# Moving one block of second multilayer products and its output norm from the next-to-last stage into the last stage of a graph layer kernel

## The chip, the cores and the metric

One core of one Trainium2 chip runs the whole program. The metric is the time of the program on the device in microseconds. The kernel before takes 388.86 us (median of three runs, 388.27 to 390.04).

## The reference, cut to what matters

Thirty-two graphs of 256 tokens with 128 features pass through two layers. Each adds its input and normalises over the features:

```
L0: h      = bn2(conv17(relu(bn1(conv1(x)))));  x_conv = relu(h + x)
    A      = exp(-|s_n - s_m|^2), s = x @ w_se.T + b_se;  x_nmp = A @ relu(x @ w_msg.T + b_msg)
    r, z   = sigmoid(...), n = tanh(...)        # gates from x_conv, x_nmp and x
    x1     = layernorm(x + (1 - z) * n + z * x)
L1: hidden = relu(((1 + eps) * x1 + adj @ x1) @ W1 + b1)
    x2     = layernorm(x1 + hidden @ W2 + b2)
```

The kernel masks A with adj. Everything is float32. The products that need its precision split each operand into a high and a low part and take three matmuls in place of one.

## The kernel before, in words

The graphs are worked in 8 groups of 4 (GROUPS, GB). A group has 1024 columns (4 graphs by 256 tokens), in two halves h = 0 and 1 of 512 columns, which fill one PSUM bank each. The eight banks are `fb` (two, "front"), `bb` (three, "back") and `cb` (three, "conv").

The order on each engine is written out by hand: `run` (line 416) calls `prologue`, then `steady(s, u, front)` for s = 1 to 7, then `last`. Stage s works on three groups at once. For `gb = s - 1` it does the back part: gates, first norm, aggregation, both multilayer products, second norm, store. For `gm = s` it does the front part: convolution, distances and `nmp`. For `gf = s + 1` it prepares the streams of the convolution. The loop of stages 2 to 5 is a hardware loop. Stage 7 has `front=False`: there is no group 8 to prepare. `last` does the back part of group 7. It cuts that group into three items (LAST_ITEMS): the whole half 0, and the two quarters (256 columns) of half 1. That shortens the chain at the end.

The names that the change touches, with the lines of the profile:

- `mlp2(g, h)` on TensorE (L1424) is the second multilayer product: 4 blocks by 2 halves of the hidden units, 8 matmuls in the code for each half of the group, which the trace shows as 16 instructions of 128x128. It writes the bank "out" from the tile `hid`, which is part of the tensor `tail`.
- `nmp(g, h)` on TensorE (L1335, tiles front<-amat,msg) is the message product. It needs the masked matrix (`mask` on POOL, L542) and the tile `msg`. `nmp_high` on ACT (L619) and `nmp_low` on DVE (L821) split its result into nmph and nmpl.
- `gates(g, u, h, c)` on TensorE (L1222): six matmuls of r from x and nmp, three of hn, three more of r from the convolution, nine of z and six of n. The r products wait for `nmp_low` (NL_READY). The convolution part of r waits for both `xconv_low` on DVE (L967, XCL_READY), the low part of relu(x + conv). That follows `inf_add` (L962) and `xconv_high` on ACT (L694).
- `add_b2` on POOL (L536) writes xn + b2 into `ot`, which is the last part of `tail`. `out_stats` on DVE adds the bank "out" (L1025), takes the statistics (L991, two instructions of 256 columns) and the variance (L995). `rsqrt` on POOL (L524) and `out_shift` on DVE (L1039) follow, then `out_norm` on ACT (L703, one instruction for each of 4 blocks) and `store` on SP (L456).
- `aggregate` (L1335, tiles adjT,xn), `y_transpose` (L1386), `y_apply` (L1013), `h_high`, `h_low` (L619, L821) and `hidden` (ACT L710) are steps of the last group around the moved work.

Engines wait only on counting semaphores, and each executes its own queue in order. In stage 7, TensorE's queue ends with `mlp2(6, 0)`, `mlp2(6, 1)`, `nmp(7, 0)`, `nmp(7, 1)`. DVE's ends with

```
pair1_add(gm, 0); pair1_add(gm, 1); out_stats(gb, 0); xconv_low(gm, 0); out_stats(gb, 1)
nmp_low(gm, 0); inf_add(gm); nmp_low(gm, 1); xconv_low(gm, 1); out_shift(gb, 0); out_shift(gb, 1)
```

Of the kernel before, what the change touches and what calls it, by code (L numbers as in the profile page):

```python
# [11 lines left out]
EPS = 1e-5  # L12
# [83 lines left out]
def gnn_kernel(nc, t, out):  # L96
# [10 lines left out]
    with ctx:  # L107
# [70 lines left out]
        stats = sb("stats", [P, 2, PAIRS, BLK, 3])  # L178
        rstd = sb("rstd", [P, 2, PAIRS, BLK])
        shift = sb("shift", [P, PAIRS, BLK])  # L180
# [261 lines left out]
        def _(sp):  # L442
# [6 lines left out]
            def store(g, h, c=None):  # L449
# [6 lines left out]
                done(sp.dma_start(dst, ot[:, h, q, :].rearrange("p (b r) d -> p b (r d)", r=PAR)), STORED[h])  # L456
# [18 lines left out]
            def steady(s, u, front):  # L475
# [20 lines left out]
        def _(pool):  # L496
# [35 lines left out]
            def add_b2(g, h, c=None):  # L532
                q = slice(part_blocks(c).start, part_blocks(c).stop)
                wait(pool, XN_READY, g, item(h, c) + 1)
                wait(pool, STORED[h], g - 1, 16)
                done(pool.tensor_tensor(ot[:, h, q, :], xn[:, h, q, :],  # L536
# [44 lines left out]
            def steady(s, u, front):  # L581
# [15 lines left out]
                rsqrt(1, gb, 1)  # L597
# [3 lines left out]
            def last(g, u):  # L601
# [15 lines left out]
        def _(act):  # L617
# [82 lines left out]
            def out_norm(g, h, c=None):  # L700
                wait(act, SHIFT_READY, g, item(h, c) + 1)
                for q in part_blocks(c):
                    last = act.activation(ot[:, h, q, :], ot[:, h, q, :], ACT.Identity, bias=shift[:, h, q:q + 1],  # L703
                                          scale=rstd[:, 1, h, q:q + 1])
                done(last, OT_READY)
# [57 lines left out]
            def steady(s, u, front):  # L763
# [38 lines left out]
            def last(g, u):  # L802
# [16 lines left out]
        def _(dve):  # L819
# [167 lines left out]
            def norm_stats(k, g, h, c, src):  # L987

                q0, q1 = part_blocks(c).start, part_blocks(c).stop
                for q in range(q0, q1, 2):  # L990
                    last = dve.bn_stats(stats[:, k, h, q:q + 2, :].rearrange("p q s -> p (q s)"),  # L991
# [3 lines left out]
                done(dve.tensor_scalar(rstd[:, k, h, q0:q1], stats[:, k, h, q0:q1, 2], 1.0 / D, (4 * EPS, EPS)[k],  # L995
# [6 lines left out]
            def out_block(h):  # L1002
                return lambda a, b: ot[:, h, a:b, :].rearrange("p q d -> p (q d)")
# [5 lines left out]
            def y_apply(g, h, c=None):  # L1009
                src = y_block(h, c)  # L1010
                wait(dve, RSTD[0], g, item(h, c) + 1)
                for q in part_blocks(c):
                    last = dve.tensor_scalar(xn[:, h, q, :], src(q, q + 1), stats[:, 0, h, q, 1:2], rstd[:, 0, h, q:q + 1],  # L1013
# [7 lines left out]
            def out_stats(g, h, c=None):  # L1021
                wait(dve, W2_FULL, g, item(h, c) + 1)
                wait(dve, XNB_READY, g, item(h, c) + 1)
                row = ot[:, h, :, :].rearrange("p k d -> p (k d)")[:, part(c)]
                done(dve.tensor_tensor(row, bank("out", h, c), row, ALU.add), V_READY)  # L1025
                wait(dve, V_READY, g, item(h, c) + 1)
                norm_stats(1, g, h, c, out_block(h))

            def out_apply(g, h, c):
                wait(dve, RSTD[1], g, item(h, c) + 1)  # L1030
                for q in part_blocks(c):
                    last = dve.tensor_scalar(ot[:, h, q, :], ot[:, h, q, :], stats[:, 1, h, q, 1:2],
                                             rstd[:, 1, h, q:q + 1], ALU.subtract, ALU.mult)
                done(last, LAST_READY)

            def out_shift(g, h, c=None):
                q = slice(part_blocks(c).start, part_blocks(c).stop)
                wait(dve, RSTD[1], g, item(h, c) + 1)
                done(dve.scalar_tensor_tensor(shift[:, h, q], stats[:, 1, h, q, 1], -1.0, rstd[:, 1, h, q],  # L1039
# [96 lines left out]
            def steady(s, u, front):  # L1136
# [36 lines left out]
                out_stats(gb, 0)  # L1173
                xconv_low(gm, 0)
                if front:
                    half_stream(gf)
# [4 lines left out]
                out_stats(gb, 1)  # L1181
                nmp_low(gm, 0)
                inf_add(gm)
                if front:
                    stream_low(gf, 2)
                nmp_low(gm, 1)
                xconv_low(gm, 1)
                out_shift(gb, 0)
                out_shift(gb, 1)

            def last(g, u):
# [12 lines left out]
                for h, c in LAST_ITEMS:  # L1204
                    h_low(g, h, c)
# [11 lines left out]
        def _(pe):  # L1217
# [128 lines left out]
            def gates(g, u, h, c=None):  # L1346
# [14 lines left out]
                if i == 0:  # L1361
                    wait(pe, V_READY, g - 1, 2)
# [39 lines left out]
            def mlp1(g, h, c=None):  # L1402
                i = item(h, c)
                for f in range(2):
# [135 lines left out]
```

How the kernel before makes its waits and increments, by code:

```python
        def wait(eng, name, g, j):  # L321
            s, per, first, missing = count[name]
            v = (g - first) * per + j - missing
            if not (isinstance(v, int) and v <= 0):
                eng.wait_ge(s, v)
# [131 lines left out]
            def prologue():  # L458
                sp.dma_start(first_w[:, :], t["first"]).then_inc(first_loaded, 16)
                sp.dma_start(xv[0][:, cols(0)], x_v[0, :, cols(0)]).then_inc(x_pair0_loaded, 16)
                done(sp.dma_start(xv[0][:, cols(1)], x_v[0, :, cols(1)]), X_LOADED)
                sp.dma_start(c2raw[:, 0:5, :], t["conv2"][:, 0:5, :]).then_inc(conv2_loaded, 16)
                sp.dma_start(c2raw[:, 5:9, :], t["conv2"][:, 5:9, :]).then_inc(conv2_loaded, 16)
                sp.dma_start(later_w[:, :], t["later"]).then_inc(later_loaded, 16)
                sp.wait_ge(conv2_loaded, 64)
                wait(sp, X_LOADED, 0, 16)
                load_x(1, 1)
                load_adj(0, 0)
                sp.dma_start(graw, t["gates"]).then_inc(gates_loaded, 16)
                wait(sp, A_READY, 0, 1)
                wait(sp, CONV_FULL[MINUS1], 0, 1)
                sp.wait_ge(w_low, w_count(MINUS1))
                load_adj(1, 1)
# [78 lines left out]
            def prologue():  # L552
# [7 lines left out]
                pool.memset(full(facthl[:, :, :, :]), 0.0).then_inc(factors_set, 1)  # L560
                pool.memset(fact[:, :, :, :], 1.0).then_inc(factors_set, 1)
                pool.wait_ge(exponent_set, 1)
                pool.wait_ge(bn_var_ready, 1)
```

## Time and profile before

| what | value |
|---|---|
| median of three runs | 388.86 us |
| the profiled execution's own time | 390.09 us |
| span of the profiled execution, first to last instruction | 388.3 us |
| TensorE (PE) busy | 363.9 us, 94% of the span |
| VectorE (DVE) busy | 327.9 us, 84% |
| ScalarE (ACT) busy | 231.5 us, 60% |
| GpSimd (POOL) busy | 223.3 us, 58% |
| mean granted TensorE clock | 0.986 of full speed |

The span leaves out 1.8 us of the execution's own time, before the first and behind the last instruction. The busy times overlap. Stage 7 ends and `last` begins at about 355 us of the span.

### The profile page before, as it was taken

The page shows a single profiled execution, that of the slowest core. Times are in us where ns is not written, and L with a number is a line of the kernel's source. Part 1 is how long each engine was busy: PE and PEld are TensorE (multiplying, and loading weights), DVE is VectorE, ACT ScalarE, POOL GpSimd, SP SyncE. Part 2 cuts the span into 40 slices and gives each one's busy share as a digit, 9 for nine tenths or more (in the row PEclk, how much of TensorE's full clock was granted, in tenths as well). Part 3 has the DMA queues.
Part 4 walks back from the last instruction along what each step waited for, and adds up shares of the span by engine and source line. Part 5 has one row for each costly group of instructions (what it writes and reads, how often), then busy time and mean ns, then how long its engine had stood idle before and what let it go on. Part 6 is the DMA issues. An engine that isn't in the chain of part 4 may idle for free.

```text
span 388.3 us, 6417 instructions
## 1 busy us (share of the span) xinstructions
PE 363.9 (94%) x2150; PEld 314.4 (81%) x2150; DVE 327.9 (84%) x669; ACT 231.5 (60%) x435; POOL 223.3 (58%) x195
## 2 busy tenths in 40 slices
PE   4969998899999999999999999999999999999974
PEld 1747866798888998989888898989888898988953
DVE  3999999999699986999689986999789986977564
ACT  4455345563866566673775667674676558472773
POOL 3346173698428763597437863597537863395342
PEclk9998998999999999999999999999999999999998
DMA  6500003130110210120100300130101201000011
GB/s 231 223 0 3 0 0 114 51 111 1 56 54 18 93 43 13 56 108 0 54 23 31 108 27 27 54 108 0 57 5 50 110 2 54 3 0 2 0 56 54
DMA packets 7991, 19.39 MB, mean 50 GB/s; under 512 B 672, under 2 KB 5024, under 8 KB 6944
## 3 DMA queue, kind: packets, MB, share of 16 engines
q1 hardware_dynamic: 7536, 18.50, 13.6%
q10 hardware_dynamic: 432, 0.59, 0.4%
q8 instruction: 13, 0.21, 0.2%
q14 instruction: 10, 0.08, 0.1%
HBM read 14.90 MB, written 4.19 MB: 49 GB/s over the span
## 4 chain that ended last, share of the span: by engine, by line
PE 60%; DVE 30%; issue 5%; DMA 2%; ACT 1%; POOL 1%; SPq 0%; DVEq 0%; ACTq 0%
PE back L1222 25%; PE conv L1222 17%; PE back L1335 6%; PE back L1424 3%; DVE stats L991 3%; DVE stl L821 3%; DVE tail L1025 2%; PE front L1307 2%; DMA tail<-in_conv_dram 2%; DVE nmpl L821 2%; DVE adjT L1087 2%; DVE wl L1044 2%; PE back L1386 2%; DVE sv L842 1%; PE front L1327 1%
## 5 line engine op out<-in xcount | busy, mean ns | idle before, releaser
L1222 PE MATMUL conv<-sth,wh 128*128 128x256 f32 x217 | 65.4, 301 | 2.0 <-DVE stl L821 1.9
L1222 PE MATMUL conv<-stl,wh 128*128 128x256 f32 x217 | 61.8, 285 | 0.0
L1222 PE MATMUL conv<-sth,wl 128*128 128x256 f32 x217 | 61.7, 284 | 0.0
L524 POOL TENSOR_TENSOR rstd<-rstd,minus_half 128x4 f32<-128x4 f32 (+1 forms) x34 | 38.7, 1138 | 34.0 <-DVE rstd L995 33.4
L542 POOL TENSOR_TENSOR amat<-amat,adjT 128x512 f32<-128x512 f32 x32 | 50.4, 1604 | 4.6 <-ACT amat L663 4.6
L529 POOL TENSOR_TENSOR xw<-xw,xv 128x512 f32<-128x512 f32 (+1 forms) x17 | 21.4, 1256 | 50.0 <-ACT xw L687 50.0
L1222 PEld LDWEIGHTS conv<-sth,wh 128*128 128x128 f32 x217 | 40.9, 189 | 4.7 <-DVE stl L821 1.8
L1222 PEld LDWEIGHTS conv<-stl,wh 128*128 128x128 f32 x217 | 41.0, 189 | 0.1
L1222 PEld LDWEIGHTS conv<-sth,wl 128*128 128x128 f32 x217 | 40.8, 188 | 0.0
L619 ACT ACTIVATE sth<-sv 128x272 fp32r<-128x272 f32 (+1 forms) x33 | 17.3, 523 | 33.6 <-DVE sv L842 21.5
L536 POOL TENSOR_TENSOR tail<-xn,later_w 128x512 f32<-128x512 f32 (+1 forms) x17 | 30.8, 1815 | 4.3 <-DMA out_dram<-tail 2.6
L550 POOL TENSOR_TENSOR adjT<-adjT,diag 128x256 f32<-128x256 f32 x32 | 28.4, 917 | 8.0 <-DVE diag L1133 8.0
L703 ACT ACTIVATE tail<-tail,shift,rstd 128x128 f32<-128x128 f32 x62 | 24.8, 481 | 12.7 <-DVE shift L1039 12.7
L510 POOL TENSOR_TENSOR sv<-vv 128x272 f32<-128x272 f32 x8 | 9.1, 1143 | 35.1 <-DVE vv L869 35.1
L1335 PE MATMUL front<-amat,msg 128*128 128x256 f32 x128 | 29.1, 379 | 0.0
L1335 PE MATMUL back<-adjT,xn 128*128 128x256 f32 x120 | 28.2, 387 | 0.8 <-DVE xn L1013 0.8
L1424 PEld LDWEIGHTS back<-later_w,tail 128*128 128x128 f32 x240 | 28.0, 192 | 0.6
L1424 PE MATMUL back<-later_w,tail 128*128 128x128 f32 x240 | 28.1, 275 | 0.0
L1335 PEld LDWEIGHTS front<-amat,msg 128*128 128x128 f32 x128 | 23.8, 190 | 2.9
L1335 PEld LDWEIGHTS back<-adjT,xn 128*128 128x128 f32 x120 | 22.0, 190 | 5.1 <-DVE xn L1013 1.5
L710 ACT ACTIVATE tail<-back,first_w 128x512 f32<-128x512 f32 (+1 forms) x30 | 20.5, 682 | 9.2 <-PE back L1222 8.9
L957 DVE TENSOR_TENSOR usum<-usum,pm 128x512 f32<-128x512 f32 x16 | 25.4, 1624 | 0.0
(225 smaller groups left out, 1028.1 us busy)
## 6 DMA issues: line engine op xcount, KB each, us to landing
adjT<-in_adj_dram SPq DMA_DIRECT2D x8, 1024.0 KB, 4.8
out_dram<-tail SPq DMA_DIRECT2D x15, 256.0 KB, 2.2
xv<-in_x_dram SPq DMA_DIRECT2D x7, 512.0 KB, 3.3
gbuf<-in_gates_dram SPq DMA_DIRECT2D x1, 576.0 KB, 6.5
tail<-in_conv_dram ACTq DMA_DIRECT2D x2, 256.0 KB, 3.7
xv<-in_x_dram SPq DMA_DIRECT2D x2, 256.0 KB, 5.0
later_w<-in_later_dram SPq DMA_DIRECT2D x1, 452.0 KB, 7.2
tail<-in_conv_dram SPq DMA_DIRECT2D x1, 320.0 KB, 5.3
```

Of the source, the lines that this page charges most:

```text
L524: done(pool.tensor_tensor(rstd[:, k, h, q], rstd[:, k, h, q], minus_half[:, q], ALU.pow), RSTD[k])
L529: done(pool.tensor_tensor(xw[:, h, part(c)], xw[:, h, part(c)], xv[u][:, part_cols(h, c)], ALU.mult), XWX_READY)
L536: done(pool.tensor_tensor(ot[:, h, q, :], xn[:, h, q, :], b2bc.unsqueeze(1).to_broadcast([P, len(part_blocks(c)), D]), ALU.add), XNB_READY)
L542: done(pool.tensor_tensor(amat[:, b, :, :], amat[:, b, :, :], adjT[u][:, b, :, :], ALU.mult), A_READY)
L550: done(pool.tensor_tensor(dg, dg, diag[:, :].unsqueeze(1).to_broadcast([P, PAR, P]), ALU.add), ADJE_READY)
L703: last = act.activation(ot[:, h, q, :], ot[:, h, q, :], ACT.Identity, bias=shift[:, h, q:q + 1], scale=rstd[:, 1, h, q:q + 1])
L710: done(act.activation(hid[:, h, f, part(c)], bank("hid", h, c, f), ACT.Relu, bias=vec[:, B1 + f:B1 + f + 1]), HID_READY)
L821: done(dve.tensor_tensor(dst, src, full(hi), ALU.subtract), name)
L957: done(dve.tensor_tensor(a, a, p1, ALU.add), PRE_READY)
L1222: ins = pe.matmul(bank, a, b, start=first and k == 0, stop=last and k == len(todo) - 1)
L1335: ins = pe.matmul(tile[:, k * N:(k + 1) * N], lhs(b, rm), rhs(b, rm), start=rm == 0, stop=rm == PAR - 1)
L1424: ins = pe.matmul(bank("out", h, c)[:, k * P:(k + 1) * P], hid[:, h, f, q * P:(q + 1) * P], w2[:, f, :], start=f == 0, stop=f == 1)
```

## The change

Half 1 of group 6 gives up its place in stage 7 for all that follows its hidden layer. Its second product (`mlp2`) is issued in `last`, behind the gates of group 7 and one transpose, and goes to the bank `cb[0]`. The final add, the statistics, the square root, the norm and the store of that half move into `last` as well. In stage 7 the two `xconv` splits and `inf_add` of group 7 come ahead of the add of half 0, and ahead of the `nmp` splits.

So that the output tile of half 1 stays with group 6 until it is stored, the two quarters of half 1 of group 7 get their output in the tile `msg`, which is free once `nmp(7)` is done, and a third row in `stats`, `rstd` and `shift`. These three tiles grow by 96, 32 and 16 bytes in each partition.

The diff, cut to its core:

```diff
-        stats = sb("stats", [P, 2, PAIRS, BLK, 3])          # rstd, shift likewise
+        stats = sb("stats", [P, 2, PAIRS + 1, BLK, 3])
+        def place(h, c):
+            return PAIRS if h == 1 and halved(c) else h
+        def held_back(g, h):
+            return isinstance(g, int) and g == GROUPS - 2 and h == 1
+        def out_tile(h, c):
+            return msg[:, :, :, :].rearrange("p r b d -> p (r b) d")[:, 0:BLK, :] if place(h, c) == PAIRS else ot[:, h, :, :]
 # SP
                 store(gb, 0)
-                store(gb, 1)
+                if front:
+                    store(gb, 1)
             def last(g, u):
+                store(g - 1, 1)
                 for h, c in LAST_ITEMS:
 # POOL
             def add_b2(g, h, c=None):
-                wait(pool, STORED[h], g - 1, 16)
+                if place(h, c) == h:
+                    wait(pool, STORED[h], g - 1, 16)
+                else:
+                    wait(pool, NMP_FULL, g, 2)
-                rsqrt(1, gb, 1)                             # steady
+                if front:
+                    rsqrt(1, gb, 1)
                     add_b2(g, h, c)                         # last
+                rsqrt(1, g - 1, 1)
 # ACT, steady
-                nmp_high(gm, 0)
                 if front:
+                    nmp_high(gm, 0)
                     stream_high(gf, 2)
-                nmp_high(gm, 1)
-                xconv_high(gm, 1)
+                    nmp_high(gm, 1)
+                    xconv_high(gm, 1)
+                else:
+                    xconv_high(gm, 1)
+                    nmp_high(gm, 0)
+                    nmp_high(gm, 1)
 # ACT, last
                 out_norm(g - 1, 0)
-                h_high(g, 0, WHOLE)
-                out_norm(g - 1, 1)
-                h_high(g, 1, 0)
-                h_high(g, 1, 1)
+                for h, c in LAST_ITEMS:
+                    h_high(g, h, c)
                 for h, c in LAST_ITEMS:
                     hidden(g, h, c)
+                out_norm(g - 1, 1)
 # DVE, steady, front=False
+                    inf_add(gm)
+                    xconv_low(gm, 0)
+                    xconv_low(gm, 1)
+                    out_stats(gb, 0)
+                    nmp_low(gm, 0)
+                    nmp_low(gm, 1)
+                    out_shift(gb, 0)
 # DVE, last
-                for h, c in LAST_ITEMS:
-                    h_low(g, h, c)
+                h_low(g, 0, WHOLE)
+                out_sum(g - 1, 1)
+                h_low(g, 1, 0)
+                h_low(g, 1, 1)
+                out_norm_stats(g - 1, 1)
+                out_shift(g - 1, 1)
 # PE
                 if i == 0:                                  # gates, before hn
-                    wait(pe, V_READY, g - 1, 2)
+                    wait(pe, V_READY, g - 1, 2 if c is None else 1)
+                    if c == WHOLE and f == 1:               # mlp1, before the second half of item 0
+                        wait(pe, V_READY, g - 1, 2)
                 wait(pe, HID_READY, g, 2 * i + 2)           # mlp2
+                if held:
+                    wait(pe, TZ_READY, g + 1, 3)
+                tile = cb[0] if held else bank("out", h, c)
                 mlp2(gb, 0)                                 # steady
-                mlp2(gb, 1)
+                if front:
+                    mlp2(gb, 1)
                 gates(g, u, 1, 1)                           # last
                 y_transpose(g, 1, 0)
+                mlp2(g - 1, 1)
                 aggregate(g, u, 0, WHOLE, (0,))
```

`out_sum` is the add of `out_stats`, and `out_norm_stats` the rest of it.

## Rows read from the trace of the kernel before

**Rows 1.** The page's first part: busy time of each engine.
```profile
PE 363.9 (94%) x2150; PEld 314.4 (81%) x2150; DVE 327.9 (84%) x669; ACT 231.5 (60%) x435; POOL 223.3 (58%) x195
```
**Rows 2.** The chain that ended last, 318 to 389 us: start, us, what.
```profile
348.17 3.57 PE back L1424 x32
```
**Rows 3.** Timeline of TensorE, 348 to 358 us: start, us, engine, line, operation.
```profile
348.01 3.73 PE L1424 MATMUL back<-later_w,tail 128*128 128x128 f32 x32
...
351.58 3.62 PE L1335 MATMUL front<-amat,msg 128*128 128x256 f32 x16
...
354.98 0.47 PE L1222 MATMUL back<-xh,wh 128*128 128x512 f32 x1
...
356.91 0.39 PE L1222 MATMUL back<-xh,wl 128*128 128x512 f32 x1
...
357.67 0.50 PE L1222 MATMUL back<-xch,wh 128*128 128x512 f32 x1 [0.37 <-DVE xcl L967]
```
**Rows 4.** Timeline of all engines, 368 to 372 us.
```profile
368.44 0.47 ACT L683 ACTIVATE gbuf<-conv,gbias 128x256 f32<-128x256 f32 x1 [0.58 <-PE conv L1222]
...
368.96 0.38 PE L1386 MATMUL conv<-ident_w,gbuf 128*128 128x128 f32 x2
...
369.50 1.36 DVE L1013 TENSOR_SCALAR xn<-back,stats,rstd 128x128 f32<-128x128 f32 x4
...
370.96 1.10 PE L1335 MATMUL front<-adjT,xn 128*128 128x256 f32 x4 [1.62 <-issue]
```
**Rows 5.** Timeline of DVE, 344 to 358 us.
```profile
350.00 0.69 DVE L1025 TENSOR_TENSOR tail<-back,tail 128x512 f32<-128x512 f32 x1 [2.76 <-PE back L1424]
...
351.60 0.69 DVE L967 SCALAR_TENSOR_TENSOR xcl<-usum,xch 128x512 fp32r<-128x512 f32 x1
...
354.14 0.69 DVE L821 TENSOR_TENSOR nmpl<-front,nmph 128x512 fp32r<-128x512 f32 x1 [0.26 <-ACT nmph L619]
...
356.48 1.14 DVE L967 SCALAR_TENSOR_TENSOR xcl<-usum,xch 128x512 fp32r<-128x512 f32 x1
```
**Rows 6.** Timeline of ACT, 348 to 354 us.
```profile
348.80 0.62 ACT L694 ACTIVATE xch<-usum 128x512 fp32r<-128x512 f32 x1
353.51 0.60 ACT L619 ACTIVATE nmph<-front 128x512 fp32r<-128x512 f32 x1 [4.09 <-PE front L1335]
```
**Rows 7.** Timeline of POOL, 341 to 358 us.
```profile
341.14 2.60 POOL L536 TENSOR_TENSOR tail<-xn,later_w 128x512 f32<-128x512 f32 x1 [0.24 <-DVE xn L1013]
343.70 5.93 POOL L542 TENSOR_TENSOR amat<-amat,adjT 128x512 f32<-128x512 f32 x4
351.77 1.39 POOL L524 TENSOR_TENSOR rstd<-rstd,minus_half 128x4 f32<-128x4 f32 x1 [2.14 <-DVE rstd L995]
...
354.94 3.27 POOL L550 TENSOR_TENSOR adjT<-adjT,diag 128x256 f32<-128x256 f32 x4
```
**Rows 8.** Timeline of all engines, 374 to 385 us.
```profile
374.09 1.27 POOL L536 TENSOR_TENSOR tail<-xn,later_w 128x512 f32<-128x512 f32 x1 [0.36 <-DMA out_dram<-tail]
...
376.33 0.42 DVE L821 TENSOR_TENSOR nmpl<-back,nmph 128x256 fp32r<-128x256 f32 x1 [0.29 <-ACT nmph L619]
...
376.41 0.39 PE L1222 MATMUL conv<-nmph,w1h 128*128 128x512 f32 x1
...
380.14 0.69 DVE L1025 TENSOR_TENSOR tail<-front,tail 128x512 f32<-128x512 f32 x1 [3.39 <-PE front L1424]
...
380.88 0.47 ACT L710 ACTIVATE tail<-back,first_w 128x256 f32<-128x256 f32 x1
...
383.17 2.41 ACT L703 ACTIVATE tail<-tail,shift,rstd 128x128 f32<-128x128 f32 x6 [1.82 <-DVE shift L1039]
```
**Rows 9.** The page's DMA issues: KB each, us from issue to landing.
```profile
out_dram<-tail SPq DMA_DIRECT2D x15, 256.0 KB, 2.2
```
**Rows 10.** The page's groups, weight loads: count | busy us, mean ns | idle before.
```profile
L1222 PEld LDWEIGHTS conv<-sth,wh 128*128 128x128 f32 x217 | 40.9, 189 | 4.7 <-DVE stl L821 1.8
...
L1424 PEld LDWEIGHTS back<-later_w,tail 128*128 128x128 f32 x240 | 28.0, 192 | 0.6
```

More of the change, by code:

```diff
@@ L701, in out_norm @@
                 wait(act, SHIFT_READY, g, item(h, c) + 1)
+                o, v = out_tile(h, c), place(h, c)
                 for q in part_blocks(c):
-                    last = act.activation(ot[:, h, q, :], ot[:, h, q, :], ACT.Identity, bias=shift[:, h, q:q + 1],
-                                          scale=rstd[:, 1, h, q:q + 1])
+                    last = act.activation(o[:, q, :], o[:, q, :], ACT.Identity, bias=shift[:, v, q:q + 1],
+                                          scale=rstd[:, 1, v, q:q + 1])
                 done(last, OT_READY)
@@ L989, in norm_stats @@
                 q0, q1 = part_blocks(c).start, part_blocks(c).stop
+                v = place(h, c)
                 for q in range(q0, q1, 2):
-                    last = dve.bn_stats(stats[:, k, h, q:q + 2, :].rearrange("p q s -> p (q s)"),
+                    last = dve.bn_stats(stats[:, k, v, q:q + 2, :].rearrange("p q s -> p (q s)"),
                                         src(q, q + 2).rearrange("p (q d) -> p d q", q=2))
@@ L1019, in h_low, with out_sum, out_norm_stats, out_stats @@
                 low(hl[:, h, part(c)], bank("agg", h, c), hh[:, h, part(c)], HL_READY)
-            def out_stats(g, h, c=None):
+            def out_sum(g, h, c=None):
                 wait(dve, W2_FULL, g, item(h, c) + 1)
                 wait(dve, XNB_READY, g, item(h, c) + 1)
-                row = ot[:, h, :, :].rearrange("p k d -> p (k d)")[:, part(c)]
-                done(dve.tensor_tensor(row, bank("out", h, c), row, ALU.add), V_READY)
+                row = out_tile(h, c).rearrange("p k d -> p (k d)")[:, part(c)]
+                src = cb[0][:, :] if held_back(g, h) else bank("out", h, c)
+                done(dve.tensor_tensor(row, src, row, ALU.add), V_READY)
+            def out_norm_stats(g, h, c=None):
                 wait(dve, V_READY, g, item(h, c) + 1)
-                norm_stats(1, g, h, c, out_block(h))
+                norm_stats(1, g, h, c, out_block(h, c))
+            def out_stats(g, h, c=None):
+                out_sum(g, h, c)
+                out_norm_stats(g, h, c)
             def out_apply(g, h, c):
                 wait(dve, RSTD[1], g, item(h, c) + 1)
+                o, v = out_tile(h, c), place(h, c)
                 for q in part_blocks(c):
-                    last = dve.tensor_scalar(ot[:, h, q, :], ot[:, h, q, :], stats[:, 1, h, q, 1:2],
-                                             rstd[:, 1, h, q:q + 1], ALU.subtract, ALU.mult)
+                    last = dve.tensor_scalar(o[:, q, :], o[:, q, :], stats[:, 1, v, q, 1:2], rstd[:, 1, v, q:q + 1],
+                                             ALU.subtract, ALU.mult)
                 done(last, LAST_READY)
@@ L1037, in out_shift @@
                 q = slice(part_blocks(c).start, part_blocks(c).stop)
+                v = place(h, c)
                 wait(dve, RSTD[1], g, item(h, c) + 1)
-                done(dve.scalar_tensor_tensor(shift[:, h, q], stats[:, 1, h, q, 1], -1.0, rstd[:, 1, h, q],
+                done(dve.scalar_tensor_tensor(shift[:, v, q], stats[:, 1, v, q, 1], -1.0, rstd[:, 1, v, q],
                                               ALU.mult, ALU.mult), SHIFT_READY)
@@ L1180, in steady @@
                     stream_low(gf, 1)
[L1181 to L1184, printed above, removed]
+                    out_stats(gb, 1)
+                    nmp_low(gm, 0)
+                    inf_add(gm)
                     stream_low(gf, 2)
[L1186 to L1189, printed above, removed]
+                    nmp_low(gm, 1)
+                    xconv_low(gm, 1)
+                    out_shift(gb, 0)
+                    out_shift(gb, 1)
+                else:
+                    inf_add(gm)
+                    xconv_low(gm, 0)
+                    xconv_low(gm, 1)
+                    out_stats(gb, 0)
+                    nmp_low(gm, 0)
+                    nmp_low(gm, 1)
+                    out_shift(gb, 0)
             def last(g, u):
@@ L1418, in mlp2 @@
                 i = item(h, c)
+                held = held_back(g, h)
                 wait(pe, HID_READY, g, 2 * i + 2)
[L1420 removed]
+                if held:
+                    wait(pe, TZ_READY, g + 1, 3)
+                elif c is not None:
                     wait(pe, (XN_READY, HL_READY, HID_READY)[i], g, (3, 3, 1)[i])
+                tile = cb[0] if held else bank("out", h, c)
                 for k, q in enumerate(part_blocks(c)):
                     for f in range(2):
[L1424 removed]
+                        ins = pe.matmul(tile[:, k * P:(k + 1) * P], hid[:, h, f, q * P:(q + 1) * P],
                                         w2[:, f, :], start=f == 0,
```

25 lines of the change are left out of this document (11 added, 14 removed).

## The prediction

> **What bounds the kernel now.** I began with the busy times [rows 1]: TensorE has 94% of the span, so work off its queue pays only where it has no hole to go into. The chain of waits came next [rows 2]. It holds the 32 instructions of the two second products of group 6, in front of the message product and the gates of group 7. Later it passes through all engines, to the last norms on ACT. The timelines of the two seams follow. TensorE at the start of the last group [rows 3]: it runs without a hole to 356.91, then stands for DVE's xcl. TensorE behind the last gates [rows 4]: two transposes at 368.96, then 1.62 us of nothing, until DVE has made xn (369.50 + 1.36 = 370.86). So there are 1.8 us of work ahead of the seam that needs no place there, and a hole of nearly that length 20 us later. The other engines' timelines [rows 5 to 7] say whether they can follow.
>
> **Part 1: the second product leaves stage 7.** The 32 instructions start at 348.01 and the message product at 351.58 [rows 3]: 3.57 / 32 = 0.112 us each. Sixteen go: 1.79 us. Is the message product free to start 1.79 us earlier, at 349.79? Its first half needs two masks and its second all four. POOL's four masks end at 343.70 + 5.93 = 349.63 [rows 7]. Yes. It takes 354.98 - 351.58 = 3.40 us [rows 3], so TensorE reaches the gates at 353.19.
>
> The gates' first products need the low part of the first message half. ACT makes the high part from 353.51 now [rows 6], so from 351.72, and ends it at 352.32. What is ahead of nmp_low on DVE is new: ACT's two xch (348.80 and 349.3, 0.62 each) let xcl start at about 349.45, and two xcl of 0.69 end at 350.74. Then out_stats, the add with its statistics and variance, holds DVE for 1.6 us (350.00 to 351.60), to 352.3 [rows 5]. nmp_low then ends at about 352.40 + 0.69 = 353.09, 0.1 us before TensorE asks. That is thin: 0 to 0.3 us could be lost here. Term: -1.79.
>
> **Part 2: the stall goes.** The gates' matmuls start (356.91 - 354.98) / 8 = 0.24 us apart, so the convolution part would start at 357.15. It starts at 357.67, and that first matmul after the pause takes 0.50 and not 0.39 [rows 3]: 0.52 + 0.11 = 0.63 us. With inf_add and both xcl ahead of out_stats, xcl is ready at 350.74, and TensorE comes to it at 353.19 + 9 x 0.24 = 355.35. The wait is over 4.6 us early, so the whole 0.63 goes. Next late would be the first message half, counted in part 1. The wait ahead of hn falls from two adds to one; that one ends at 351.4. Term: -0.63. Bounds: -0.63, or 0 if nmp_low takes the place of xcl.
>
> The second xcl takes 1.14 us and the first 0.69, of the same shape; during the second, POOL adds the diagonals (354.94 to 358.21) [rows 5, 7]. In the new order both xcl come before that work, but the first (349.45) meets the end of the last mask (349.63). At most 0.2 us is added to DVE's queue, and nmp_low slips by up to 0.1 us behind TensorE. The Trainium skill (SBUF — State Buffer, Who interferes with whom) says that a DVE instruction with two SBUF inputs contends with a GpSimd instruction that reads SBUF, and that whoever is first holds the pair for the whole instruction. By that rule the first xcl starts at 349.63; the trace agrees in the 1.14 against 0.69. The moved add reads PSUM and the statistics have one input, so by the same rule they don't slow POOL.
>
> **Part 3: the product in its new place.** It stands behind the two transposes and waits for tz of the last item, which ACT ends at 368.44 + 0.47 = 368.91, before the transposes start [rows 4]. So the wait is met. Nothing else is behind it but the aggregation, which waits for 370.86 anyway. In the times of before, the product starts at about 369.18, and 16 x 0.112 = 1.79 us later TensorE is free: 370.97, against 370.96 at which the aggregation starts now. Term: 0. Bounds: -0.1 (the aggregation's first matmul comes without a pause, as the 0.11 of part 2) to +0.3 (the slot is 1.62 and its edges are not sharp). If the cover were gone altogether it would be +1.79.
>
> **Part 4: the norm of the held half** (in times of before; the whole block shifts alike). DVE: the 0.69 us add goes between the low splits of items 0 and 1. At the worst it pushes the last split from 376.33 + 0.42 = 376.75 to 377.4, while TensorE has the second half of mlp1 of item 0 in front of it, from 376.41 for three matmuls of 0.24 [rows 8]. That second half waits for the add too, which stands behind one split of 0.69 [rows 5] and ends near 375.8. So mlp1 of item 1 may come 0.1 late, where TensorE still has slack: 0. Statistics and variance follow in some 0.9 us (1.6 less the add), to 377.7 or at worst 378.3; DVE stands until 380.14 [rows 8]. POOL: the add of item 0 ends at 374.09 + 1.27 = 375.36. The two quarter adds behind it no longer wait for the store and take as much together, to 376.6, or to 378.0 at the 2.60 of rows 7. The square root (1.39 [rows 7]) of the variance at 377.7 ends at 379.1 (at worst 379.7), the shift 0.2 later: before 380.14. ACT: the norm (4 x 0.40, from 2.41 / 6) goes behind the last hidden (380.88 + 0.47 = 381.35) and ends at 382.95. The chain asks for ACT at 383.17 [rows 8]: 0.2 us are spare. Term: 0; bounds 0 to +1.6 (ACT's four on the path). The norm's old place, among the high splits of group 7, is counted at nothing as well: TensorE waits for xn there.
>
> SP: the store of the held half goes ahead of the last three, issued at 383.0. SP's next issue is due when the norm of item 0 ends, at 383.17 + 4 x 0.40 = 384.8. The first lands 2.2 us later [rows 9], at 385.2, as the data of the next store begin. Term: 0; bounds 0 to +0.3. POOL's new wait, for the message product, is met: that ends before the gates start.
>
> **The sum.** -1.79 - 0.63 + 0 + 0 = -2.42 us. The profiled execution took 390.09, with a span of 388.3: it would be 387.7 and 385.9. That execution is 1.23 above the median of the three runs; on the median, 388.86 - 2.42 = 386.4. I say 386.5, for the 0.1 us that part 1 may lose. What a measurement can tell here is 0.5%, 1.94 us: the forecast is -0.62%, not far beyond it.
>
> **Rivals.**
> 1. *DVE becomes the bound at the seam.* nmp_low is behind two xcl and a whole out_stats now. If xcl take 1.14 each, and one waits for the mask, DVE is 1.1 later, nmp_low ends at 354.1, and TensorE stands 0.9 us (and 0.1 for the restart): 388.86 - 2.42 + 1.0 = 387.4. For it: only 0.1 us of slack. Against it: no POOL work besides the last 0.2 us of the mask.
> 2. *The tail takes it back.* The norm of the held half ends on the path: ACT's four instructions stand before the last norms. With all 1.6 us: 388.0. For it: 0.2 us of slack, and a wait of DVE on POOL ahead of the add of item 0. Against it: every step above fits with POOL at double time.
> 3. *The hole isn't a hole.* The product delays the aggregation in full: 388.86 - 0.63 = 388.2. Or the message product can't start earlier (masks): 388.2 as well. Against: 368.91, 370.86 and 349.63.
> 4. *Slower: the grown tiles.* xn and tail start 144 bytes later in each partition, in every stage, not only in the last. TensorE loads weights from tail in 240 instructions of 192 ns [rows 10]. If each took 10% more and it came through to the end, 240 x 0.019 = 4.6 us: 388.86 - 2.42 + 4.6 = 391.0. It decides from 2.42 / 240 = 10 ns on. Against: loads from another tensor take 189 ns, 3 ns less, so the place in memory shows little so far; but no row has the same tensor at two places.
>
> **Chances.** Forecast (-2.0 to -2.7): 0.68. Rival 1: 0.12 at full price. Rival 2: 0.10. Rival 3: 0.06. Rival 4: 0.04. The range 386.0 to 387.9 holds the forecast's, rival 1 and half of rival 2. Faster by over 0.5%: 0.72 (the forecast and a light form of rivals 1 and 2). Within 0.5%: 0.24. Slower: 0.04.
>
> **What would show it.** The message product follows 16 instructions of L1424 and starts near 349.8. No DVE xcl wait stands in front of TensorE at the gates, which start near 353.2, and their convolution part near 355.4. The other 16 of L1424 stand at about 366.8 with the aggregation right behind (about 368.6). The four L703 of the held half end before the shift of item 0, and the span is 385.9. I am wrong if nmpl releases TensorE at the gates by more than 0.3 us, if the aggregation comes over 0.3 us behind xn, or if ACT's first L703 of item 0 is started by ACT itself and not by DVE's shift. Gaps in stages 1 to 6 would mean rival 4.

## The result, and the profile after

The changed kernel takes 386.50 us (median of 6 runs, 386.14 to 386.63) against 389.07 us for the kernel before, run beside it (6 runs). The ratio is 0.993, with a 95% interval of 0.9918 to 0.9942: faster by 0.7%. The prediction was 386.5 us. The profiled execution took 386.43 us, with a span of 384.5 us. One run of all those reported here, one of e7 below, was in a slower state of the chip (408.35 us, granted clock 0.847) and is left out of its median.

The lines have moved: L1222, L1335, L1386, L1424 of before are L1266, L1379, L1430, L1474 now, and DVE's L967 and L1025 are L990 and L1050. The busy times hardly differ from [rows 1], since no work was removed:

```profile
PE 363.2 (94%) x2150; PEld 315.1 (82%) x2150; DVE 326.4 (85%) x669; ACT 232.1 (60%) x435; POOL 222.5 (58%) x195
```

The chain of waits has 16 instructions of L1474 ahead of the message product where [rows 2] has 32. The 21 matmuls of the gates behind it (r, hn and z of item 0) are one piece of TensorE: before, the chain left TensorE there for ACT's nmph and DVE's nmpl and xcl.

```profile
346.82 1.78 PE back L1474 x16
348.60 3.46 PE front L1379 x16
352.06 4.90 PE back L1266 x21
```

**The first seam**, which is where stage 7 hands over to the last group. The timeline of TensorE, to be read against [rows 3]. To compare two traces I take times from the start of the masks of group 7 on POOL, the last thing ahead of the change. It is 343.70 before [rows 7] and 342.35 here.

```profile
346.66 1.95 PE L1474 MATMUL back<-later_w,tail 128*128 128x128 f32 x16
348.44 3.62 PE L1379 MATMUL front<-amat,msg 128*128 128x256 f32 x16
351.83 0.47 PE L1266 MATMUL back<-xh,wh 128*128 128x512 f32 x1
...
354.01 0.39 PE L1266 MATMUL back<-xch,wh 128*128 128x512 f32 x1
```

| step of TensorE, from the masks' start | before | after | difference |
|---|---|---|---|
| message product starts | 7.88 | 6.09 | -1.79 |
| gates start | 11.28 | 9.48 | -1.80 |
| convolution part of r starts | 13.97 | 11.66 | -2.31 |
| first aggregation starts | 27.26 | 24.86 | -2.40 |
| end of the span | 44.57 | 42.17 | -2.40 |

There is no idle time in brackets at 354.01, and that matmul takes 0.39 and not 0.50. The timeline of DVE there, against [rows 5]:

```profile
345.99 0.48 DVE L985 SCALAR_TENSOR_TENSOR usum<-conv,sc,usum 128x256 f32<-128x256 f32 x1
348.10 1.33 DVE L990 SCALAR_TENSOR_TENSOR xcl<-usum,xch 128x512 fp32r<-128x512 f32 x2 [1.62 <-ACT xch L713]
349.35 0.68 DVE L1050 TENSOR_TENSOR tail<-back,tail 128x512 f32<-128x512 f32 x1
...
351.00 0.69 DVE L844 TENSOR_TENSOR nmpl<-front,nmph 128x512 fp32r<-128x512 f32 x1
```

Both xcl are done at 349.43, 4.6 us before TensorE wants them. nmpl ends at 351.69, and TensorE starts the gates at 351.83, 0.14 us later. That is not time to spare, as e5 shows below: in that run TensorE stands idle for nmpl, and it starts as far behind its end. nmpl itself starts 0.03 us behind the end of ACT's nmph (350.97), as in all traces but that of e5. POOL and ACT beside them, against [rows 6, 7]:

```profile
342.35 5.93 POOL L559 TENSOR_TENSOR amat<-amat,adjT 128x512 f32<-128x512 f32 x4
...
352.10 2.84 POOL L567 TENSOR_TENSOR adjT<-adjT,diag 128x256 f32<-128x256 f32 x4
```

```profile
350.37 0.60 ACT L638 ACTIVATE nmph<-front 128x512 fp32r<-128x512 f32 x1 [1.78 <-PE front L1379]
```

**The second seam**, behind the last gates. The timeline of all engines at the hole of [rows 4]. The product fills it. xn is ready at 367.10 (365.74 + 1.36), and the aggregation starts at 367.21, 0.11 us behind it. Before it was 0.10 us.

```profile
365.20 0.38 PE L1430 MATMUL conv<-ident_w,gbuf 128*128 128x128 f32 x2
...
365.42 1.95 PE L1474 MATMUL conv<-later_w,tail 128*128 128x128 f32 x16
...
365.74 1.36 DVE L1037 TENSOR_SCALAR xn<-back,stats,rstd 128x128 f32<-128x128 f32 x4
...
367.21 1.10 PE L1379 MATMUL front<-adjT,xn 128*128 128x256 f32 x4
```

**The tail**, the norms and stores at the end. The timeline of all engines, against [rows 8].

```profile
371.25 0.68 DVE L1050 TENSOR_TENSOR tail<-conv,tail 128x512 f32<-128x512 f32 x1
...
371.50 1.44 POOL L553 TENSOR_TENSOR msg<-xn,later_w 128x256 f32<-128x256 f32 x2
...
372.57 0.42 DVE L844 TENSOR_TENSOR nmpl<-back,nmph 128x256 fp32r<-128x256 f32 x1 [0.31 <-ACT nmph L638]
...
373.96 1.02 POOL L538 TENSOR_TENSOR rstd<-rstd,minus_half 128x4 f32<-128x4 f32 x1 [1.02 <-DVE rstd L1019]
375.01 0.16 DVE L1072 SCALAR_TENSOR_TENSOR shift<-stats,rstd 128x4 f32<-128x4 f32 x1 [1.13 <-POOL rstd L538]
...
377.47 1.64 ACT L723 ACTIVATE tail<-tail,shift,rstd 128x128 f32<-128x128 f32 x4
...
379.39 1.65 ACT L723 ACTIVATE tail<-tail,shift,rstd 128x128 f32<-128x128 f32 x4 [0.29 <-DVE shift L1072]
...
381.83 0.85 SPq L467 DMA_DIRECT2D out_dram<-msg  x2
```

The held half's add (371.25) doesn't move the last low split: it starts 372.57 - 342.35 = 30.22 behind the masks and 376.33 - 343.70 = 32.63 before, 2.41 earlier like all the rest. DVE waits 1.13 us for POOL's root and has the shift at 375.17, 1.2 us before the add of item 0 (376.38). ACT ends the held norm and still waits 0.29 us for DVE's shift of item 0. From start to start there is more: ACT's norms of one row follow each other 0.38 us apart, so item 0 could start at 377.47 + 1.54 = 379.01, and starts at 379.39. That is 0.38 to 0.39 us to spare.

**What is not of the change.** The two profiled spans (388.27 and 384.52) differ by 3.75 us, 2.40 of them behind the masks' start. The other 1.35 are there from the start-up on. The first stores of the two, in SP's timeline, are 1.31 apart, before first:

```profile
98.37 1.93 SPq L456 DMA_DIRECT2D out_dram<-tail  x2
```

```profile
97.06 1.93 SPq L467 DMA_DIRECT2D out_dram<-tail  x2
```

From there to the masks both take 245.3 us. The experiments, whose code is the same up to stage 7 (e3 and all kernels with the change have the three tiles grown), show this start-up anywhere in between, and beyond. The granted clock is not what moves it: its mean is 0.998 in e10, whose masks start 1.06 us later than those of this profile with 0.989. What moves it stays open. From 340 to 381 us the granted clock is 1.00 in all thirteen traces.

### The profile page after: what moved, and what is told of

Read it like the earlier page. It is cut to its first block, busy times and chain, and to the rows that moved or that the text cites. A ratio compares the mean times of both kernels' runs of the same rounds, so it can differ in the third digit from the quotient of the medians.

```text
span 384.5 us, 6418 instructions
## 1 busy us (share of the span) xinstructions
PE 363.2 (94%) x2150; PEld 315.1 (82%) x2150; DVE 326.4 (85%) x669; ACT 232.1 (60%) x435; POOL 222.5 (58%) x195
## 4 chain that ended last, share of the span: by engine, by line
PE 61%; DVE 30%; issue 5%; DMA 1%; ACT 1%; POOL 1%; SPq 0%; DVEq 0%; ACTq 0%
PE back L1266 26%; PE conv L1266 17%; PE back L1379 6%; DVE stats L1015 3%; PE back L1474 3%; DVE stl L844 3%; DVE tail L1050 2%; PE front L1351 2%; DVE wl L1077 2%; DVE adjT L1120 2%; PE back L1430 2%; DVE sv L865 1%; DVE nmpl L844 1%; DMA tail<-in_conv_dram 1%; PE front L1371 1%
## 5 line engine op out<-in xcount | busy, mean ns | idle before, releaser
L1266 PE MATMUL conv<-sth,wh 128*128 128x256 f32 x217 | 65.4, 301 | 1.9 <-DVE stl L844 1.8
L1266 PE MATMUL conv<-stl,wh 128*128 128x256 f32 x217 | 61.8, 285 | 0.0
L1266 PE MATMUL conv<-sth,wl 128*128 128x256 f32 x217 | 61.7, 284 | 0.0
L1266 PEld LDWEIGHTS conv<-sth,wh 128*128 128x128 f32 x217 | 40.9, 189 | 4.6 <-DVE stl L844 1.7
L1266 PEld LDWEIGHTS conv<-stl,wh 128*128 128x128 f32 x217 | 41.1, 189 | 0.1
L1266 PEld LDWEIGHTS conv<-sth,wl 128*128 128x128 f32 x217 | 40.8, 188 | 0.0
L553 POOL TENSOR_TENSOR tail<-xn,later_w 128x512 f32<-128x512 f32 x15 | 29.4, 1959 | 2.0 <-DVE xn L1037 1.7
L1379 PE MATMUL front<-amat,msg 128*128 128x256 f32 x128 | 29.1, 379 | 0.0
L1379 PE MATMUL back<-adjT,xn 128*128 128x256 f32 x120 | 28.2, 387 | 0.8 <-DVE xn L1037 0.8
L1474 PEld LDWEIGHTS back<-later_w,tail 128*128 128x128 f32 x224 | 26.2, 192 | 0.6
L1474 PE MATMUL back<-later_w,tail 128*128 128x128 f32 x224 | 26.3, 275 | 0.0
L1379 PEld LDWEIGHTS front<-amat,msg 128*128 128x128 f32 x128 | 23.8, 190 | 2.9
L1379 PEld LDWEIGHTS back<-adjT,xn 128*128 128x128 f32 x120 | 22.0, 190 | 5.1 <-DVE xn L1037 1.5
```

Of the source, the lines that this page charges most:

```text
L553: done(pool.tensor_tensor(out_tile(h, c)[:, q, :], xn[:, h, q, :], b2bc.unsqueeze(1).to_broadcast([P, len(part_blocks(c)), D]), ALU.add), ...
L1266: ins = pe.matmul(bank, a, b, start=first and k == 0, stop=last and k == len(todo) - 1)
L1379: ins = pe.matmul(tile[:, k * N:(k + 1) * N], lhs(b, rm), rhs(b, rm), start=rm == 0, stop=rm == PAR - 1)
L1474: ins = pe.matmul(tile[:, k * P:(k + 1) * P], hid[:, h, f, q * P:(q + 1) * P], w2[:, f, :], start=f == 0, stop=f == 1)
```

## The experiments

The measure is the distance from the start of the masks of group 7 to the end of the span, in one profiled execution each; the median of the timed runs stands beside it. "The kernel after" in the diffs is the changed kernel.

| kernel | masks start | first aggregation, from the masks | end, from the masks | median us (runs) |
|---|---|---|---|---|
| before | 343.70 | 27.26 | 44.57 | 389.07 (6) |
| after | 342.35 | 24.86 | 42.17 | 386.50 (6) |
| e1, reorder only | 343.60 | 26.65 | 43.95 | 388.61 (12) |
| e2, product only | 343.06 | 25.47 | 42.76 | 387.27 (6) |
| e3, grown tiles | 342.88 | 27.27 | 44.56 | 389.13 (12) |
| e4, product twice | 342.98 | 26.64 | 43.70 | 388.52 (12) |
| e5, DVE later | 342.65 | 25.97 | 43.27 | 387.62 (4) |
| e6, norm earlier | 342.92 | 24.85 | 42.16 | 386.76 (4) |
| e7, norm twice | 344.15 | 24.86 | 43.31 | 387.97 (7) |
| e8, last quarters on DVE | 343.19 | 24.81 | 41.89 | 386.62 (6) |
| e9, a quarter of the product | 343.90 | 24.83 | 42.14 | 387.16 (4) |
| e10, the changed kernel again | 343.41 | 24.84 | 42.14 | 386.30 (5) |
| e11, e8 again | 342.72 | 24.84 | 41.91 | 386.13 (5) |

The kernel before ran beside them all, with medians of 389.01 to 389.11. Two traces of one kernel agree in the distance within 0.03 us (after and e10, e8 and e11). The masks' start varies by 1.8 us, and medians of one kernel differ by 0.2 us (after and e10) and 0.5 us (e8 and e11), so the distance decides where a few tenths matter.

**e1: the order of stage 7 alone.**

```diff
 # the kernel before, ACT and DVE in stage 7 (front=False)
+                    xconv_high(gm, 1); nmp_high(gm, 0); nmp_high(gm, 1)
+                    inf_add(gm); xconv_low(gm, 0); xconv_low(gm, 1)
+                    out_stats(gb, 0); out_stats(gb, 1); nmp_low(gm, 0); nmp_low(gm, 1)
```

> The kernel before, with only the order of ACT and DVE in stage 7 changed: inf_add and both xconv splits first, both out_stats next, the nmp splits last. The second product of half 1 stays in stage 7. Distance from the start of the masks of group 7 on POOL to the end of the span (44.6 us before, 42.15 after the change). My theory: the wait of TensorE for xcl goes and nothing else, so 0.63 us less, 43.95, with no pause ahead of the gates' convolution part; in the time, 0.6 us less, too small for a verdict. Rival (the nmp splits behind the out_stats become the wait): the gates start late by 0.5 us or more and the distance stays at 44.6.

Measured: 43.95, 0.62 us less than before; the time's ratio is 0.9988 (0.9978 to 0.9998). DVE's timeline shows both xcl ahead of the two adds. The second term of the sum stands alone, at its size.

```profile
349.36 1.32 DVE L971 SCALAR_TENSOR_TENSOR xcl<-usum,xch 128x512 fp32r<-128x512 f32 x2 [1.63 <-ACT xch L694]
350.60 0.68 DVE L1029 TENSOR_TENSOR tail<-back,tail 128x512 f32<-128x512 f32 x1
```

**e2: the product alone.**

```diff
 # the kernel after, ACT and DVE in stage 7
-                    xconv_high(gm, 1); nmp_high(gm, 0); nmp_high(gm, 1)
+                    nmp_high(gm, 0); nmp_high(gm, 1); xconv_high(gm, 1)
-                    inf_add; xconv_low 0; xconv_low 1; out_stats 0; nmp_low 0; nmp_low 1
+                    out_stats 0; xconv_low 0; nmp_low 0; inf_add; nmp_low 1; xconv_low 1
```

> The kernel after, with the old order of ACT and DVE in stage 7 (out_stats, xconv 0, nmp 0, inf_add, nmp 1, xconv 1). The product stays moved. My theory: the message product and the gates start 1.79 us earlier than before relative to the masks, but TensorE waits again for the second xcl, which now overlaps the diagonals on POOL and takes 1.1 us and not 0.67. TensorE reaches the convolution part 11.66 us behind the masks' start, xcl is done about 12 to 12.6 behind it: a pause of 0.4 to 1.0 us. Distance 42.6 to 43.2 instead of 42.15. Rival (the new order is not needed once the product is gone, since DVE has one out_stats less): 42.15, no pause.

Measured: 42.76, which is 1.81 less than before and 0.59 more than after. The rival fails: TensorE waits for xcl as before. TensorE's timeline, then DVE's and POOL's:

```profile
355.23 0.50 PE L1266 MATMUL back<-xch,wh 128*128 128x512 f32 x1 [0.36 <-DVE xcl L990]
```

```profile
350.96 0.69 DVE L990 SCALAR_TENSOR_TENSOR xcl<-usum,xch 128x512 fp32r<-128x512 f32 x1
...
354.05 1.12 DVE L990 SCALAR_TENSOR_TENSOR xcl<-usum,xch 128x512 fp32r<-128x512 f32 x1
```

```profile
352.50 3.27 POOL L567 TENSOR_TENSOR adjT<-adjT,diag 128x256 f32<-128x256 f32 x4
```

The xcl that falls beside the diagonals takes 1.12 us, against 1.14 in [rows 5]. The diagonals took 3.27 here and before, but 2.84 in the kernel after, where no xcl falls on them: each holds up the other. The two parts add up: 0.62 + 1.81 = 2.43, and both together gave 2.40.

**e3: the grown tiles.**

```diff
-        stats = sb("stats", [P, 2, PAIRS, BLK, 3])
+        stats = sb("stats", [P, 2, PAIRS + 1, BLK, 3])     # rstd, shift likewise; nothing else
```

> The kernel before, with only the three tiles grown (stats, rstd, shift by 96, 32 and 16 bytes in a partition), so that xn and tail start 144 bytes later. My theory: no difference, the distance 44.6 and the time within 0.3 us of before, weight loads of L1424 at 192 ns. Rival 4 of the prediction: slower loads, a longer time. Second rival: the 1.3 us by which the profiled run of the changed kernel is ahead already before stage 7 comes from the place in memory; then this kernel is 1.3 us faster than before.

Measured: 44.56 and a ratio of 1.0002 (0.9993 to 1.0011). Both rivals fail. The weight loads of L1424 take 192 ns at either place. The start-up of this kernel is 0.8 us ahead of the first profile of before, with no gain in the median.

**e4: the product twice.**

```diff
-                for k, q in enumerate(part_blocks(c)):
+                for k, q in [kq for _ in range(2 if held else 1) for kq in enumerate(part_blocks(c))]:
```

> The kernel after, with the held product issued twice in its slot (32 instructions in place of 16; the second 16 write the same values again). My theory: the slot of 1.8 us is full with 16, so the aggregation starts 1.79 us later and the end comes 1.6 to 1.8 us later, distance 43.8 to 43.95. Rival (the chain behind the aggregation has slack, or the product costs nothing wherever it stands): under 0.5 us.

Measured: the first aggregation 1.78 us later and the end 1.53 later, a little under the 1.6 that I had as the least. TensorE's timeline shows the slot full and where 0.2 us comes back: the pause ahead of the quarters' aggregation is 0.54 and no longer 0.76.

```profile
366.04 3.74 PE L1474 MATMUL conv<-later_w,tail 128*128 128x128 f32 x32
369.62 1.03 PE L1379 MATMUL front<-adjT,xn 128*128 128x256 f32 x4
...
372.27 2.01 PE L1379 MATMUL back<-adjT,xn 128*128 128x256 f32 x8 [0.54 <-DVE xn L1037]
```

**e9: a quarter of the product.** Three of its four blocks are left out of the computation.

```diff
-                for k, q in enumerate(part_blocks(c)):
+                for k, q in list(enumerate(part_blocks(c)))[:1 if held else None]:
```

> The kernel after, with a quarter of the held product in its slot: 4 of the 16 instructions, the other three blocks of that half are left out of the computation. My theory: the aggregation behind it waits for xn anyway, so removing 1.34 us of work from the slot moves it by 0.1 us at most, distance from the masks to the end 42.1 to 42.2 as with all 16. Rival 3 of the prediction in a weak form (the full product already delays the aggregation by a few tenths): 41.9 or less.

Measured: 42.14, against 42.17 and 42.14 with the whole product. With e4 this bounds the slot from both sides: 12 instructions fewer give 0.01 to 0.03 us at the aggregation, 16 more cost 1.78 us there. The width of the slot can be read here, from the start of the product to that of the aggregation: 368.73 - 366.95 = 1.78 us, and the whole product takes 367.21 - 365.42 = 1.79 us. It is full to about 0.01 us. The idle time is back ahead of the aggregation:

```profile
366.95 0.61 PE L1474 MATMUL conv<-later_w,tail 128*128 128x128 f32 x4
368.73 1.10 PE L1379 MATMUL front<-adjT,xn 128*128 128x256 f32 x4 [1.17 <-issue]
```

**e5: DVE later at the first seam.**

```diff
                     xconv_low(gm, 1)
+                    for _ in range(2):
+                        dve.scalar_tensor_tensor(shadow[:, _, :, :], pre[:, :, 1, :], 0.0, full(xch[:, :, 1, :]), ...)
                     out_stats(gb, 0)
```

> The kernel after, with two more DVE instructions of xcl's form ahead of out_stats in stage 7; their results go to a tile that nobody reads. In the profile of the change the low part of the first message half ended at 351.69 and TensorE began the gates at 351.83, 0.14 us later. My theory (rival 1 of the prediction is real but was 0.14 us away): 2 x 0.63 us more on DVE make TensorE wait for nmpl at the gates, 1.26 - 0.14 + 0.1 for the restart = 1.2 us; distance from the masks to the end 43.3 to 43.4 instead of 42.15. Rival (DVE has more slack there than 0.14, or the loss is won back later): 42.15 to 42.8.

Measured: the gates start 353.27 - 342.65 = 10.62 behind the masks, 1.14 later than after, and the end is at 43.27, 1.10 later, just under the 43.3 that I had as the least. TensorE's timeline names the wait:

```profile
353.27 0.47 PE L1270 MATMUL back<-xh,wh 128*128 128x512 f32 x1 [0.90 <-DVE nmpl L845]
```

DVE's timeline shows what was added and where it went:

```profile
349.65 1.28 DVE L1228 SCALAR_TENSOR_TENSOR shadow<-usum,xch 128x512 f32<-128x512 f32 x2
350.85 0.68 DVE L1051 TENSOR_TENSOR tail<-back,tail 128x512 f32<-128x512 f32 x1
...
352.44 0.69 DVE L845 TENSOR_TENSOR nmpl<-front,nmph 128x512 fp32r<-128x512 f32 x1
```

The add behind the two extra instructions starts 350.85 - 342.65 = 8.20 behind the masks and not 7.00, so they took 1.20 us of DVE and not the 1.26 that I had used. nmpl starts 9.79 behind the masks and not 8.65, 1.14 later. So DVE had 0.06 us to spare: nmpl starts 0.14 us behind the start of the variance (rstd) there, waiting for ACT's nmph, and 0.08 us here. All the rest came through to the gates.

TensorE had nothing to spare. Here, where it stood idle for nmpl, it starts 0.15 us behind the end of nmpl (353.13). The same interval is 0.14 to 0.15 us in all thirteen traces: 351.69 to 351.83 after, and 354.83 to 354.98 before [rows 3, 5]. It is the time from a release to the start. The message product's last matmul starts 0.16 us ahead of the gates in all traces but this one, so TensorE and nmpl come to the gates together.

**e6: the held norm earlier.**

```diff
-                for h, c in LAST_ITEMS:
+                for h, c in LAST_ITEMS[:-1]:
                     hidden(g, h, c)
                 out_norm(g - 1, 1)
+                hidden(g, *LAST_ITEMS[-1])
```

> The kernel after, with the held norm on ACT ahead of the hidden layer of the last item instead of behind it. ACT stands idle there for 1.77 us and the shift is ready 0.2 us into that, so the last hidden starts at most 0.1 us later. My theory: the end is set by DVE's shift of item 0, so nothing changes, distance 42.1 to 42.25, and ACT's idle time before the norm of item 0 grows from 0.29 to over 1.5 us. Rival 2 of the prediction (the held norm is on the path at the tail): 0.3 us or more less.

Measured: 42.16, nothing. ACT's timeline: the norm fits in the idle time, and 1.82 us of idle time, released by DVE's shift, stand ahead of item 0.

```profile
375.77 1.65 ACT L723 ACTIVATE tail<-tail,shift,rstd 128x128 f32<-128x128 f32 x4 [0.24 <-DVE shift L1073]
...
379.97 1.65 ACT L723 ACTIVATE tail<-tail,shift,rstd 128x128 f32<-128x128 f32 x4 [1.82 <-DVE shift L1073]
```

**e7: the held norm twice.**

```diff
+                if held_back(g, h):
+                    for q in part_blocks(c):
+                        act.activation(xw[:, h, q * D:(q + 1) * D], o[:, q, :], ACT.Identity, ...)
```

> The kernel after, with four more ACT instructions of the held norm's form behind the last hidden, whose results go to a tile that nobody reads any more. ACT has 0.29 us to spare before the norm of item 0. My theory: 4 x 0.41 - 0.29 = 1.35 us later, distance 43.5. Rival (the last stores, not ACT, set the end, so that part of it is hidden): 43.0 or less.

Measured: 43.31, 1.14 later and not 1.35. ACT is on the path now: the held norm and that of item 0 are one row without idle time. The four added take 380.81 - 379.28 = 1.53 us back to back (0.38 each, where I had used 0.41). ACT's room is to be counted from start to start, like the added work: 0.39 us, as above, and not the idle time of 0.29. 1.53 - 0.39 = 1.14. ACT's timeline:

```profile
379.28 1.64 ACT L724 ACTIVATE xw<-tail,shift,rstd 128x128 f32<-128x128 f32 x4
380.81 3.17 ACT L727 ACTIVATE tail<-tail,shift,rstd 128x128 f32<-128x128 f32 x8
```

**e8 and e11: the last quarters' norms on DVE.** With the seams settled, what is left at the end is a queue: ACT does six blocks, and SP issues two stores behind the last of them.

```diff
-                if (h, c) == LAST_ITEMS[-1]:
-                    wait(sp, LAST_READY, g, 1)
+                if halved(c):
+                    wait(sp, LAST_READY, g, c + 1)
-                for h, c in LAST_ITEMS[:-1]:
-                    out_norm(g, h, c)
+                out_norm(g, 0, WHOLE)
-                out_shift(g, 1, 0)
+                out_apply(g, 1, 0)
                 out_apply(g, 1, 1)
```

> The kernel after, with the last norm of the first quarter on DVE as well (like that of the second), so that ACT ends with item 0. DVE is idle there from 380.42 to 381.17 and the square root of that quarter is done before. My theory: the store of that quarter is issued when SP is free of item 0's, 0.35 us earlier, and the last store behind it likewise; the end comes 0.3 to 0.4 us earlier, distance 41.8. Rival (the stores are bound by the data rate, at 349 GB/s in that stretch, or DVE's two more instructions hold up the statistics of the second quarter): 0.1 us or nothing.

> The kernel of e8_last_quarters_dve beside the changed kernel on the same chip. From the traces 0.28 us less than the changed kernel, distance 41.9; in the time 386.2 against 386.5. Rival (the gain is in the trace's tail alone and no time shows it): both the same within 0.1.

Measured: 41.89 and 41.91, 0.23 to 0.28 less than the changed kernel's two traces, where I had 0.3 to 0.4. SP's last issue ends at 383.25 - 343.19 = 40.06 and not at 382.68 - 342.35 = 40.33, and the span ends 1.84 us behind it in both. On one chip the medians are 386.13 (385.85 to 386.54) against 386.30 (385.82 to 387.36) for the changed kernel: the sign agrees, but the ranges overlap, so the time alone shows no gain. In the first trial e8 had 386.62. DVE's timeline and SP's stores:

```profile
381.07 0.60 DVE L1063 TENSOR_SCALAR msg<-msg,stats,rstd 128x128 f32<-128x128 f32 x2
...
382.00 0.60 DVE L1063 TENSOR_SCALAR msg<-msg,stats,rstd 128x128 f32<-128x128 f32 x2 [0.33 <-POOL rstd L538]
382.28 0.97 SPq L467 DMA_DIRECT2D out_dram<-msg  x2
```

**e10: the changed kernel again**, without an edit.

> The changed kernel itself, beside the next one on the same chip. Both theories: 386.5, distance 42.17. The start of the masks lies anywhere from 342.3 to 344.2, as in the other profiles, which would show that the 1.35 us by which the first profile of this kernel was ahead there is of the run and not of the kernel.

Measured: 386.30, 42.14, masks at 343.41. The same code starts its masks 1.06 us later than in its first profile, and over all kernels the start lies from 342.35 to 344.15. The spread is there by the first store: 97.06 in the first profile, 98.88 in e7, whose masks start 1.80 later.

## Why the prediction was right

**Part 1, -1.79.** Measured -1.79 at the message product and -1.80 at the gates. The masks left it free, as worked out: they end at 348.28, 0.16 us before the product starts. e2 gives the part alone as 1.81. The 0.1 us that I had between nmp_low and TensorE was no spare: [rows 3, 5] have 0.15 us there already, and e5 shows that this is the time from the release to the start. What DVE could lose was 0.06 us, and what exceeds it comes through to the end. So the term held with next to nothing in hand, and closer than the prediction says.

**Part 2, -0.63.** Measured 0.51 at the convolution part and 0.09 behind it, 0.60 in all; e1 gives 0.62 alone. e2 shows that the reorder is needed even with the product gone, which the prediction had not asked.

**The extra 0.2 us on the first xcl was 0.04.** It started at 348.10, 0.18 before the last mask ended, and took 0.73 us against 0.69 of [rows 5].

```profile
347.00 1.28 POOL L559 TENSOR_TENSOR amat<-amat,adjT 128x512 f32<-128x512 f32 x1
348.10 0.73 DVE L990 SCALAR_TENSOR_TENSOR xcl<-usum,xch 128x512 fp32r<-128x512 f32 x1 [1.62 <-ACT xch L713]
```

In the kernel before, the second xcl starts at 356.48, while the third of POOL's diagonals runs, and the fourth starts while that xcl runs. POOL's timeline in short windows, which keep the two apart:

```profile
356.33 0.74 POOL L550 TENSOR_TENSOR adjT<-adjT,diag 128x256 f32<-128x256 f32 x1
...
357.02 1.19 POOL L550 TENSOR_TENSOR adjT<-adjT,diag 128x256 f32<-128x256 f32 x1
```

| trace | overlap: from the xcl's start to the end of the POOL instruction that runs | the xcl takes (0.69 alone) | added |
|---|---|---|---|
| after | 0.18 | 0.73 | 0.04 |
| e8 | 0.22 | 0.77 | 0.08 |
| e2 | 0.57 | 1.12 | 0.44 |
| before | 0.59 | 1.14 | 0.45 |

What is added is the overlap less 0.13 to 0.14 us, at the edge of a mask as in the middle of the diagonals. POOL pays in the one instruction that starts while the xcl runs: 1.19 us in place of 0.74. The rule of the Trainium skill (SBUF — State Buffer, SBUF: two separate sides), by which the one that starts first has the shared ports for its whole instruction and the other is blocked, fits both sides but for these 0.13 us. Whether they are of the instruction's end or of POOL's records, no run here shows.

**Part 3, 0.** Measured: the aggregation 0.11 behind xn, 0.10 before. e9 and e4 bound it from both sides. That the product's 1.79 us fit a hole of 1.62 is no contradiction: the idle time in the row counts from the end of the second transpose (368.96 + 0.38), while the next matmul can start 0.22 us behind the first (365.20 and 365.42 after). From start to start the slot was 370.96 - 369.18 = 1.78 us, as the prediction has it. It was a fit to about 0.01 us, and by e4 whatever more is put there comes through at the aggregation.

**Part 4, 0.** The held add pushed nothing, the shift was 1.2 us early (I had 0.8), ACT had 0.39 us to spare from start to start (I had 0.2, from ends). e6 and e7 show that this spare is all there is, and that past it the norm costs its full length. The store cost nothing: e6 issues it earlier, with the same end.

**The sum.** -2.42 forecast, -2.40 between the traces, -2.57 between the medians (386.50 and 389.07), -2.71 in the last comparison (386.30 and 389.01). That the median came out at 386.5 to the hundredth is in part luck: the kernel before has 389.07 over six runs and not the 388.86 of three that the sum started from, the 0.1 us set aside for part 1 was not needed, and the medians' difference is 0.17 us larger than that of the traces, which is within what medians of one kernel differ by. The forecast for the profiled span, 385.9, was not met by the first profile (384.5), for a reason outside of the change: 1.35 us of start-up. e10's 385.55 has 1.06 of them back.

**The rivals.** Rival 1 (DVE at the seam) was the nearest: 0.06 us away. Rival 2 was 0.39 us away. Rival 3 is out by e9 and by the message product's start at 6.09. Rival 4 is out by e3.

## What to carry to other kernels

Look for the pair: work ahead of a seam that nobody behind it needs soon, and a pause of the same engine later. Move the work there whole, and give its successors their own order in the queues that they now meet. Price each move at both of its ends. An interval between the end of one engine's work and the start of the next is no spare until a run with a forced wait shows a shorter one: count room from start to start. Here 1.79 us came from one end because the other end had a pause of that length, and 1.78 us more in the same place cost 1.5 us. Compare traces from the last event ahead of the change: the start-up moved a whole profile by up to 1.8 us here, three quarters of the gain that was to be shown.

## What the runs showed of the hardware

- The start-up is where traces of one kernel differ. SP's first load behind the weights' is issued between 8.20 us (e11) and 9.69 us (e7), the first store between 97.06 and 98.88, and from the first store to the masks of group 7 it is 245.26 to 245.36 us in all thirteen traces.
- A DVE instruction with two SBUF inputs that starts while a POOL instruction with two SBUF inputs runs is lengthened by what is left of that one, less 0.13 to 0.14 us: by 0.44 to 0.45 beside a diagonal, by 0.04 at a mask's end. The POOL instruction that starts while it runs takes 1.18 to 1.19 us and not 0.74.
- From the end of DVE's nmpl to the first gates matmul it is 0.14 to 0.15 us in all thirteen traces, from the end of xn to the aggregation 0.10 to 0.11 in all but e4. In e5 TensorE stood idle 0.90 us for nmpl; that first matmul took 0.47 us there as elsewhere. Whether it takes less where nmpl is long done, no run shows.
- At the convolution part, in the middle of an accumulation, the first matmul took 0.50 us where it had waited (before, e2) and 0.39 where it had not (after, e1).
- ACT's norms of 128x128 start 0.38 us apart in a row, though one takes 0.48 to 0.49 us, so idle time between two rows understates the room by 0.1 us.
